# Softmax weights transposed in 32x32 blocks by VectorE and ScalarE in place of TensorE, and the values product moved behind the next scores product

## The reference

```python
def _L0_xattn_ref(hidden_states, key_value_states, attention_mask, position_bias, ln_weight, w_q, w_k, w_v, w_out):
    x = _rmsnorm(hidden_states, ln_weight)
    h_q = (x @ w_q.T).reshape(b, lq, H, DH)
    h_k = (key_value_states @ w_k.T).reshape(b, lk, H, DH)
    h_v = (key_value_states @ w_v.T).reshape(b, lk, H, DH)
    score = jnp.einsum('bqhd,bkhd->bhqk', h_q, h_k) + position_bias[None]
    score = jnp.where(m, score, -jnp.inf)
    score = jax.nn.softmax(score, axis=-1)
    score = jnp.where(m, score, 0.0)
    attn = jnp.einsum('bhqk,bkhd->bqhd', score, h_v).reshape(b, lq, H * DH)
    return hidden_states + attn @ w_out.T
...
x = x + _L0_xattn_ref(_layernorm(x, axis=-1), ctx_4096, mask_BxSxS2_bk0, ...)
x = x + _L0_ffn_ref(_layernorm(x, axis=-1), ...)
x = x + _L1_xattn_ref(_layernorm(x, axis=-1), ctx_4096, ...)
x = x + _L1_ffn_ref(_layernorm(x, axis=-1), ...)
```

## Time and profile before

| | before |
|---|---|
| median of three runs | 943.76 us |
| span of the profiled execution | 942.7 us |
| TensorE busy | 933.8 us, 99% |
| TensorE weight loads | 816.1 us, 87% |
| VectorE busy | 629.9 us, 67% |
| ScalarE busy | 409.5 us, 43% |
| GpSimd busy | 520.2 us, 55% |
| granted clock of TensorE in the loop | 1.00 |
| DMA | 171.70 MB, mean 182 GB/s |

### The profile page before, as it was taken

The page is one execution under the profiler, slowest core; times in us unless marked ns, Lnnn a source line. Parts: engine busy times, 40 slices in busy tenths (PEclk is TensorE's granted clock), DMA queues, the critical chain, the costliest instruction groups (busy, mean ns, idle before and its releaser), DMA issues.

```text
span 942.7 us, 16961 instructions
## 1 busy us (share of the span) xinstructions
PE 933.8 (99%) x5517; PEld 816.1 (87%) x5517; DVE 629.9 (67%) x1161; ACT 409.5 (43%) x1143; POOL 520.2 (55%) x582
## 2 busy tenths in 40 slices
PE   9999999999999999999999999999999999999997
PEld 7888898888888888888888888988898888878885
DVE  5666664466766576756766676657665767886787
ACT  5664434344343434333434344334434344335664
POOL 3450724457565756584757565856567553133477
PEclk9999999999999999999999999999999999999999
DMA  9315327674667365745676376637673666230101
GB/s 329 110 55 177 121 116 267 215 254 153 227 228 264 119 256 197 280 150 207 221 268 204 137 268 240 212 133 279 217 271 133 224 207 224 69 123 1 35 23 68
DMA packets 61291, 171.70 MB, mean 182 GB/s; under 512 B 6056, under 2 KB 8492, under 8 KB 60989
## 3 DMA queue, kind: packets, MB, share of 16 engines
q1 hardware_dynamic: 61244, 171.11, 51.6%
HBM read 159.56 MB, written 11.53 MB: 181 GB/s over the span
## 4 chain that ended last, share of the span: by engine, by line
PE 94%; DVE 2%; ACT 1%; issue 1%; POOL 1%; DMA 1%; SPq 0%; ACTq 0%; DVEq 0%; POOLq 0%
PE ps_q L355 7%; PE ps_q L357 7%; PE ps_q L356 7%; PE ps_o L355 6%; PE ps_o L357 6%; PE ps_o L356 6%; PE ps_k L355 6%; PE ps_k L357 6%; PE ps_v L355 6%; PE ps_k L356 6%; PE ps_v L357 6%; PE ps_t L2183 6%; PE ps_v L356 6%; PE ps_s L2156 6%; PE ps_t L2173 3%
## 5 line engine op out<-in xcount | busy, mean ns | idle before, releaser
L780 ACT ACTIVATE scores<-scores,neg_max 128x128 f32<-128x128 f32 x256 | 99.8, 391 | 219.9 <-DVE neg_max L1583 219.8
L1470 DVE TENSOR_TENSOR acc<-ps_o,acc 128x512 f32<-128x512 f32 x128 | 87.8, 686 | 60.9 <-PE ps_o L357 60.9
L355 PE MATMUL ps_o<-wo_hi,att_hi 128*128 128x512 f32 x256 | 105.9, 414 | 0.0
L357 PE MATMUL ps_o<-wo_hi,att_lo 128*128 128x512 f32 x256 | 100.3, 392 | 0.0
L356 PE MATMUL ps_o<-wo_lo,att_hi 128*128 128x512 f32 x256 | 100.0, 390 | 0.0
L786 ACT COPY probs_t<-ps_t 128x512 f32<-128x512 f32 x64 | 37.7, 588 | 139.5 <-PE ps_t L2173 139.4
L1104 POOL TENSOR_TENSOR shift<-bias_sb,mask_sb 128x512 f32<-128x512 f32 x64 | 84.8, 1326 | 2.9 <-DVE scores L1579 2.9
L1458 DVE TENSOR_TENSOR att_lo<-ps_t,att_hi 128x512 fp32r<-128x512 f32 x64 | 44.2, 691 | 55.2 <-ACT att_hi L773 55.2
L1145 POOL TENSOR_TENSOR wq_lo<-raw_q,wq_hi 128x256 fp32r<-128x256 f32 x65 | 48.1, 740 | 58.9 <-ACT wq_hi L612 58.9
L355 PE MATMUL ps_v<-wv_hi,ct_hi 128*128 128x256 f32 x264 | 75.1, 284 | 0.4 <-POOL wv_lo L1125 0.3
L357 PE MATMUL ps_v<-wv_hi,ct_lo 128*128 128x256 f32 x264 | 74.7, 283 | 0.0
(11 more groups left out here) (394 smaller groups left out, 2780.9 us busy)
## 6 DMA issues: line engine op xcount, KB each, us to landing
ring_hi<-scratch_x_t SPq DMA_DIRECT2D x39, 512.0 KB, 4.0
ring_lo<-scratch_x_t SPq DMA_DIRECT2D x39, 512.0 KB, 4.9
ring_hi<-scratch_c_t SPq DMA_DIRECT2D x39, 512.0 KB, 4.0
ring_lo<-scratch_c_t SPq DMA_DIRECT2D x39, 512.0 KB, 5.3
raw_o<-in_w_o SPq DMA_DIRECT2D x16, 512.0 KB, 4.9
raw_q<-in_w_q SPq DMA_DIRECT2D x15, 512.0 KB, 6.4
raw_k<-in_w_k SPq DMA_DIRECT2D x15, 512.0 KB, 7.1
xt_hi<-scratch_x_t SPq DMA_DIRECT2D x13, 512.0 KB, 7.3
```

The source lines that it names most:

```text
L355: pe.matmul(dst, hi_l, hi_r, start=first, stop=False)
L357: return pe.matmul(dst, lo_l, hi_r, start=False, stop=last)
L780: e = act.activation(probs[n][:, m, :], scores[n][:, m, :], ACT.Exp, bias=neg_max[:, n, m:m + 1], accum_out=row_sum[:, n, m:m + 1])
L1470: dve.tensor_tensor(acc[:, b, :], ps_o[:], acc[:, b, :], ALU.add).then_inc(o_added, 1)
```

## The change

The four transposes of TensorE and `pt_evac` go. In their place `softmax_back` ends with two VectorE block transposes of the whole 128x512 tile, which turn each 32x32 block in itself. The first writes to probs_t, where the four diagonal blocks of each head are then in place. The second works in place on the weights, and from there ScalarE copies the twelve off-diagonal blocks, each 32 partitions by four heads by 32 columns, across the partitions into probs_t (`pt_blocks`). In the loop six of the copies stand where `pt_evac` stood and six behind the casts that follow. pt_out counts four times per step.

The values product of step s now waits for all four and stands on TensorE behind the scores product of step s + 1. On VectorE `attention_rest` moves behind `softmax_front`, in step c of the loop. On TensorE one more unit stands ahead of output part 0 where c is 0, 1, 2, 3 or 5. In the last two steps products of the next sub-layers move too.

```diff
+        def block_of(tile, row, col):
+            return tile[row * Q:(row + 1) * Q, :, col * Q:(col + 1) * Q]
+        def flat(tile):
+            return tile[:].rearrange("p a b -> p (a b)")
...
-                wait_from(act, pt_done, s - 1)
                 for m in range(4):
                     e = act.activation(probs[n][:, m, :], scores[n][:, m, :], ACT.Exp,
                                        bias=neg_max[:, n, m:m + 1], accum_out=row_sum[:, n, m:m + 1])
                 e.then_inc(e_done, 1)
 
-            def pt_evac(s):
-                act.wait_ge(pt_done, s + 1)
-                act.copy(probs_t[:], blocks(ps_t)).then_inc(pt_out, 1)
+            def pt_blocks(s, n, rows):
+                act.wait_ge(p_done, s + 1)
+                for i in rows:
+                    for j in range(4):
+                        if j != i:
+                            last = act.copy(block_of(probs_t, j, i), block_of(scores[n], i, j))
+                last.then_inc(pt_out, len(rows))
...
-                pt_evac(s)
+                pt_blocks(s, n, (0, 1))
...
+                pt_blocks(s, n, (2, 3))
...
+                wait_from(dve, pt_out, 4 * s - 4)
                 dve.tensor_tensor(scores[n][:], blocks(ps_s), shift[n][:], ALU.add).then_inc(s_shifted, 1)
                 dve.wait_ge(s_shifted, s + 1)
                 dve.tensor_reduce(row_max[:, n, :], scores[n][:], AX_X, ALU.max).then_inc(s_chain, 1)
-                dve.wait_ge(s_chain, 3 * s + 1)
+                dve.wait_ge(s_chain, 5 * s + 1)
                 dve.tensor_scalar(neg_max[:, n, :], row_max[:, n, :], -1.0, None, ALU.mult).then_inc(s_neg, 1)
 
             def softmax_back(s, n):
                 dve.wait_ge(e_done, s + 1)
                 dve.reciprocal(row_inv[:, n, :], row_sum[:, n, :]).then_inc(s_chain, 1)
-                dve.wait_ge(s_chain, 3 * s + 2)
+                dve.wait_ge(s_chain, 5 * s + 2)
                 dve.scalar_tensor_tensor(row_fac[:, n, :], row_max[:, n, :], -MASKED / 3.0, row_inv[:, n, :],
                                          ALU.is_gt, ALU.mult).then_inc(s_chain, 1)
-                dve.wait_ge(s_chain, 3 * s + 3)
+                dve.wait_ge(s_chain, 5 * s + 3)
                 dve.tensor_tensor(probs[n][:], probs[n][:], row_fac[:, n, :].unsqueeze(2).broadcast_to([P, 4, P]),
-                                  ALU.mult).then_inc(p_done, 1)
+                                  ALU.mult).then_inc(s_chain, 1)
+                dve.wait_ge(s_chain, 5 * s + 4)
+                dve.transpose(flat(probs_t), flat(probs[n])).then_inc(s_chain, 1)
+                dve.transpose(flat(probs[n]), flat(probs[n])).then_inc(p_done, 1)
...
@@ -1659,7 +1678,6 @@
                 summed = not (isinstance(i, int) and s < 4 * PLAIN)
                 own = not (isinstance(i, int) and i == 1)
                 coming = not last
-                attention_rest(s - 1)
                 if c % 4 == 1 and summed:
                     if not (last and c == 5):
                         q_c12(g)
@@ -1682,6 +1700,7 @@
                 if c % 4 == 3:
                     k_c11(G)
                 softmax_front(s, n)
+                attention_rest(s - 1)
...
-            def step_transpose(s, c):
-                pe.wait_ge(p_done, s + 1)
+            def step_values(s, c, made):
+                pe.wait_ge(pt_out, 4 * s + 4)
                 wait_from(pe, att_lo_s, s)
-                for m in range(4):
-                    last = pe.transpose(ps_t[:, m * P:(m + 1) * P], probs[c % 2][:, m, :], ident[:])
-                last.then_inc(pt_done, 1)
-            def step_values(s, c, made):
-                pe.wait_ge(pt_out, s + 1)
...
@@ -2395,6 +2403,14 @@
                 if not (static and s < 4 * PLAIN):
                     wait_projections(g, c)
                 step_scores(s, c)
+                if c == 0:
+                    step_values(s - 1, 7, v_count(i - 1, 14))
+                elif static and s <= 4 * PLAIN:
+                    step_values(s - 1, c - 1, s - 1 - (c - 1) % 2 + 2)
+                elif not own:
+                    step_values(s - 1, c - 1, 16)
+                else:
+                    step_values(s - 1, c - 1, v_count(i, (1, 2, 11, 12, 13, 14, 14)[c - 1]))
...
@@ -2413,18 +2429,24 @@
                     q_p4(G)
                 if last and c == 5:
                     k_p3(g)
-                output(s - 1, (c - 1) % LOOP_STEPS, g if c % 4 == 1 else None, (0,))
-                if c % 4 == 0:
+                if c == 0:
                     k_p5(g)
                 if c % 4 == 1 and more:
                     q_p6(G)
+                if c == 2:
+                    q_p2(G)
+                if c == 3:
+                    k_p4(G)
+                output(s - 1, (c - 1) % LOOP_STEPS, g if c % 4 == 1 else None, (0,))
+                if c == 4:
+                    k_p5(g)
                 if last and c == 5:
                     pe.wait_ge(v_out, v_count(i, 14))
                     for _ in range(4):
                         pe.matmul(ps_v[:, 0:P], ones[:], ones[:], start=True, stop=True)
-                if c % 4 == 2:
+                if c == 6:
                     q_p2(G)
-                if c % 4 == 3:
+                if c == 7:
...
@@ -2451,14 +2473,7 @@
                         v_p4(i, 1)
                 if c == 5 and coming:
                     v_p2(i + 1, 1)
-                step_transpose(s, c)
                 output(s - 1, (c - 1) % LOOP_STEPS, None, (1,))
-                if static and s < 4 * PLAIN:
-                    step_values(s, c, s - c % 2 + 2)
-                elif not own:
-                    step_values(s, c, 16)
-                else:
-                    step_values(s, c, v_count(i, (1, 2, 11, 12, 13, 14, 14, 14)[c]))
...
@@ -2537,13 +2552,12 @@
             s = STEPS - 2
             wait_projections(GROUPS - 1, 6)
             step_scores(s, 6)
+            step_values(s - 1, 5, v_count(TURNS - 1, 14))
             product_m(0)
             output(s - 1, 5, None, (0,))
             product_m(1)
             output(s - 1, 5, None, (1,))
-            step_transpose(s, 6)
             product_m(2)
-            step_values(s, 6, v_count(TURNS - 1, 14))
...
@@ -2558,7 +2572,7 @@
             pe.matmul(ps_v[:, 0:SL], ones[0:1, :], targets[:], start=True, stop=True).then_inc(tgt_mm, 1)
             s = STEPS - 1
             step_scores(s, 7)
-            output(s - 1, 6, None, (0,))
+            step_values(s - 1, 6, v_count(TURNS - 1, 14))
...
+            output(s - 1, 6, None, (0,))
             small_pair(0)
+            small_pair(1)
             output(s - 1, 6, None, (1,))
-            small_pair(1)
-            step_transpose(s, 7)
```

More of the change, by code:

```diff
@@ L46 @@
 MASKED = 3e38
+Q = 32
 SCORE_SCALE = float(D) ** -0.5
@@ L808, in step_first @@
                     k_evac(s + 3, (s + 3) // 2 % 2, (s + 1) % 2)
-                pt_evac(s)
+                pt_blocks(s, s % 2, (0, 1, 2, 3))
                 if s < 4:
@@ L899, in _ @@
             wk1_high_part(2)
-            pt_evac(STEPS - 4)
+            pt_blocks(STEPS - 4, 0, (0, 1, 2, 3))
             wk1_high_part(3)
@@ L912, in _ @@
             wq1_high_part(1)
-            pt_evac(STEPS - 3)
+            pt_blocks(STEPS - 3, 1, (0, 1, 2, 3))
             wq1_high_part(2)
@@ L926, in _ @@
             exponentials(STEPS - 2, 0)
-            pt_evac(STEPS - 2)
+            pt_blocks(STEPS - 2, 0, (0, 1, 2, 3))
             attention_high(STEPS - 2)
@@ L933, in _ @@
             exponentials(STEPS - 1, 1)
-            pt_evac(STEPS - 1)
+            pt_blocks(STEPS - 1, 1, (0, 1, 2, 3))
             act.wait_ge(base_in, 16)
@@ L1841, in _ @@
             weighted_rows(0, wq1_raw, 1)
-            attention_rest(STEPS - 2)
             dve.wait_ge(vec_mm, 1)
@@ L1856, in _ @@
             softmax_front(STEPS - 1, 1)
+            attention_rest(STEPS - 2)
             add_output(STEPS - 2, 6, (0,))
@@ L2364, in _ @@
                 step_scores(s, c)
+                step_values(s - 1, c - 1, s + 1 - (s - 1) % 2)
                 plain_q(s + 2, (s + 2) % LOOP_STEPS)
@@ L2376, in _ @@
             step_scores(s, 0)
+            step_values(s - 1, 7, s)
             plain_q(s + 2, 2)
```

14 lines of the change are left out of this document (3 added, 11 removed).

## The result

The changed kernel takes 1045.31 us (median of 4 runs, 1043.91 to 1047.91), the kernel before 943.68 beside it. The ratio is 1.108 with a 95% interval of 1.106 to 1.109: 10.8% slower, where I had forecast 959 us and a top of 985. The direction was right, the size was not. The profiled execution has a span of 1041.8 us, 99.1 more than the earlier trace rows.

The account below looks back on a forecast made before the run. TensorE, busy throughout the loop, was taken as the bound. 942.7 - 28.2 + 2.0 + 3.2 + 28.0 + 3.4 + 3.5 + 3.1 = 957.7, with 1.1 around it 958.8: about 959 us, range 940 to 985.

Parts of the forecast that it names:

- a top of 985: Upper end of the 8 in 10 range for the whole kernel's time, set beyond the case of dear copies.
- What goes, 28.2 us: TensorE's four transposes cost 0.44 us a step; removing all 64 groups was to gain 28.2 us in full.
- Price of a transpose, 0.60, and the add 1.31 later: Each VectorE block transpose takes 0.60 us, so the add of output part 0 to acc comes 1.31 us later.
- Which wait has little slack: Output part 1 on TensorE waits for VectorE's add; stalls of 0.33 to 1.19 in six steps, 5.3 us a turn.
- In steps 2 and 6 ScalarE does att_hi and one copy between `softmax_front` and the exponentials: 0.2.: ScalarE work placed behind the softmax's front part, delaying the end of VectorE's add by 0.2 us in these steps.
- about 0.2 each, 2.4 for twelve: Price of ScalarE's 32x128 block copies, with bounds of 0.15 and 0.39; 0.15 us lost in step 7 alone.
- my own two times, 9.95 and 9.93: Step 7: copies and what follows end at 9.95 us behind the scores; TensorE is through the next scores at 9.93.
- the rival that took the upper one (979): ScalarE's copies cost 0.39 us each; steps 7 and 3 wait 2.2 and 0.9 more, 979 us; chance 0.11.
- The weight casts on ScalarE come up to 3 us later, ahead of their use by 1.5 us or more.: In the loop, ScalarE's later weight casts were still to be ready in time; no cost was put on them.
- The clock: TensorE's granted clock, read as 1.00 in the middle of the loop.
- The sum: Span 942.7 less 28.2 for transposes, plus stalls in opening, loop and end, gives 957.7; 958.8 us with 1.1 around it.
- Outside the loop: Opening: adds hidden in steps 0 to 12, step 1 loses 2.0; end: 3.5 in step 62, 3.1 in step 63.

Follow-up runs that it names:

- a_moves: The changed kernel's new orders, but the transposes stay on TensorE and ScalarE keeps its one copy; 976.27 us.
- m_moves_khead: a_moves with the copy of ps_k2 put ahead of attention_high on ScalarE in steps 2 and 6; 954.66 us.
- g_sums: The changed kernel with three of GpSimd's four v sums in step 5 cut to 32 columns, leaving out part of the sums; 1027.40 us.
- i_split: The changed kernel with ScalarE's cast of wo_hi ahead of the second six block copies in steps 0 and 4; 1031.60 us.
- b2_dve: The kernel before with VectorE's two block transposes added in place behind the scaling, TensorE's transposes kept; 999.38 us.
- p_bank: The changed kernel with the ps_k2 copy and wo_hi cast moved earlier and output part 0 in the scores' bank ps_s; 1015.26 us.
- n_few: p_bank with four block copies a step in place of twelve, leaving out part of the work; 949.85 us.
- q_best: p_bank with q_p5 ahead of the values product in step 0, v casts ahead of the copies, and two moves in step 62; 981.90 us.

## Why the prediction was wrong

- *What goes, 28.2 us.* Right in kind: 256 matmuls are gone. TensorE's busy time rose by 2.8 us all the same, through the waits and the stretches at half clock.
- *Price of a transpose, 0.60, and the add 1.31 later.* Right (0.64 and 0.59).
- *Which wait has little slack.* Right as to place, in all six steps. My stalls are whole costs, so the 0.26 belongs to each idle time: 0.33, 0.93 and 1.19 were forecast for steps 1, 3 and 7, and 0.71, 1.22 and 1.33 came. For steps 2, 5 and 6 I had 0.97, 0.90 and 0.96, and 1.78, 2.93 and 1.83 came, which the next points explain.
- *"In steps 2 and 6 ScalarE does att_hi and one copy between `softmax_front` and the exponentials: 0.2."* This is the first step that failed. The copy is not behind `softmax_front` but ahead of it, through `k_u2`: 2.8 us late. I had looked at what the values product waits for, and not at what waits behind att_hi. Shown by a_moves and m_moves_khead; 29 us in the changed kernel.
- *A block copy "about 0.2 each, 2.4 for twelve".* Mis-sized: six take 1.83, twelve 3.66. The wait for them in front of the values product of step 7 costs 1.34 + 0.26 us, where I had 0.15 (and my own two times, 9.95 and 9.93, give only 0.02). The copy lay inside my bounds of 0.15 and 0.39, but the rival that took the upper one (979) counted only the wait of the values product.
- *"The weight casts on ScalarE come up to 3 us later, ahead of their use by 1.5 us or more."* This is the second step that failed, and it had put the late casts at nothing. I had asked whether TensorE would miss the weights; in the turn above it does once, for 0.36 us. What the late casts do besides is to move GpSimd's passes onto VectorE's neg_max, row_fac and scaling, which wait for them. Shown by g_sums (18 us) and i_split (14 us). The scaling's mean of 0.88 us in the trace of before, where such a pass alone takes 0.69, had been there to see.
- *The clock.* I had taken 1.00 throughout. It is at 0.50 for 3 us behind the 2.68 us wait of step 5, some 1.5 us a turn, and at a mean of 0.86 from 893 to 917, in step 62.
- *The sum.* Loop: forecast 10.4 us more in five turns, measured 70.1. Opening: 1.8 less, measured 7.5 more. End: 6.5 more, measured 21.6 more.
- *Outside the loop.* In the opening I had the adds hidden in steps 0 to 12; TensorE waits 0.66 and 0.24 us for them in steps 9 and 10. Its idle time for the copies of step 1 is 1.79, for which I had 2.0, but it also waits 1.19 for those of step 11, 1.47 for vv in step 0, and 0.76 to 1.31 for att_lo in steps 2, 3, 10 and 14. At the end the waits for w_rows (2.39) and for the mm casts (3.69) came where I had 3.5 and 3.1. The last turn up to step 61 takes 9.5 us more, where my terms give 0.8; step 62 takes 5.9 more and the rest 6.1, with the clock low behind both waits.

How the parts share the 99 us can't be told by adding them up: the block transposes added to the kernel before cost 55 (b2_dve), the moves alone 32, eight of the twelve copies 65 in one surrounding (p_bank to n_few) and 31.5 in another. Each engine's lateness is hidden by that of another until it is removed. No run changed the opening or the end alone, so what causes their waits is read from the trace and not shown.

## What to carry to other kernels

When a product is moved behind another, follow what stands behind its consumer in that engine's queue, not only what the product waits for: one late cast at the head of ScalarE's step held a copy that had its data, and through it the softmax. When work goes from a full engine to two half-full ones, the shares say little; here ScalarE at 43% and VectorE at 67% could not take 3.7 and 1.3 us a step on the chain from scores to values. And a later cast is not free because its reader has slack: it moves GpSimd's passes, and they can land on VectorE's.

## What the runs showed of the hardware

- A VectorE pass over 128x4 (neg_max, one input) took 1.30 us beside a GpSimd pass of 1.30 and 0.17 without it; a scaling of 128x512 took up to 1.74 in place of 0.69. The row maximum stayed at 0.69 beside a GpSimd pass (from 550.63, GpSimd's from 550.08 to 551.37), and a transpose at 0.71 (from 600.98, GpSimd's from 600.28 to 601.55). The Trainium skill (SBUF — State Buffer, SBUF: two separate sides) calls the pair of ports that both engines share an exclusive lock, held for a whole instruction. The trace agrees: neg_max and row_fac of step 5 end 0.03 and 0.02 us behind GpSimd's, and the scaling 0.55 behind.
- ScalarE's copy of a 32x128 block, gathered from four pieces of 32 columns, starts the next one after 0.305 us, no sooner than a 128x256 cast does (0.31). Partitions left unused gave nothing back: such a copy took 0.296 in the mean, a cast of 98x128 0.270.
- TensorE's granted clock was 0.50 from 559 to 562, behind 2.68 us of idle time, and back at 0.99 from 562 on; behind waits of 1.4 to 1.6 us it stayed at 1.00. Behind the wait of 1.93 in p_bank it fell in step 6 (0.54) and not in step 5 (1.00); it fell behind 1.85 us in step 0 of that turn (0.50) and stayed at 1.00 behind the 2.54 us of q_best. So in these runs the length of a wait did not settle it.
